# Identity transposes in unread PSUM banks at eight further places of a decoder stack

## What is computed

```python
# L0_ffn, two iterations of refining (names shortened)
logits = gelu(x @ w_r1 + b_r1) @ w_r2 + b_r2            # router, 8 experts, top 2
ctrl   = shared(ctx) + sum_k share_k * expert_k(ctx)    # ctx = [x, v]; alpha, beta, gate
x_next, v_next = step(ctrl, x, v, mu)
halt   = sigmoid(gelu(x_next @ w_h1 + b_h1) @ w_h2 + b_h2)
x, v   = blend by halt of x_next + iw * (gelu(x_next @ w_f1 + b_f1) @ w_f2 + b_f2)
# L1_xattn: 16 heads, each (batch, head) with a temperature from a small net
#           over mean, variance and maximum of its scores
# L1_ffn: top-1 of 14 experts: tokens sorted by expert, expert MLP, rows put back
```

## Time and profile before

| | |
|---|---|
| three timed executions | 1138.63, 1141.52, 1149.40 us (median 1141.52) |
| profiled execution, its own time | 1149.13 us |
| its span, first to last instruction | 1147.0 us |
| PE busy | 958.3 us (84%) |
| DVE, ACT, POOL busy | 749.4, 580.3, 418.2 us |
| mean granted PE clock | 0.92 of full |

### The profile page before, as it was taken

How to read it: one execution, slowest core, us unless ns; L and a number is a source line. 1 busy time by engine, 2 the same in 40 slices (tenths; PEclk the granted TensorE clock), 3 DMA queues, 4 the chain that set the end, 5 groups by cost and what they waited for, 6 DMA issues and landing times. The chain is left out here.

```text
span 1147.0 us, 27427 instructions
## 1 busy us (share of the span) xinstructions
PE 958.3 (84%) x11169; PEld 658.4 (57%) x11169; DVE 749.4 (65%) x2045; ACT 580.3 (51%) x960; POOL 418.2 (36%) x436
## 2 busy tenths in 40 slices
PE   8999899999899988988897694876657676689997
PEld 5677544444444445776686393444556565557776
DVE  4687776547756474653575143589999999646764
ACT  3565565645455435644562561476554645325442
POOL 4320300000000022776001666256778778623341
PEclk8899898999999998999797897898878888799999
DMA  7000000000000016000000223000000000000001
GB/s 277 2 3 3 20 1 1 1 1 0 1 1 1 0 62 244 3 3 2 2 3 1 84 76 117 6 1 1 2 3 3 2 2 3 2 1 2 3 2 38
DMA packets 16299, 27.98 MB, mean 24 GB/s; under 512 B 1200, under 2 KB 13616, under 8 KB 15664
## 3 DMA queue, kind: packets, MB, share of 16 engines
q1 hardware_dynamic: 14720, 23.09, 5.7%
q0 software_dynamic: 1024, 2.10, 0.6%
q10 hardware_dynamic: 432, 1.05, 0.3%
HBM read 20.33 MB, written 5.90 MB: 23 GB/s over the span
## 5 line engine op out<-in xcount | busy, mean ns | idle before, releaser
L1435 PE MATMUL l0f_ctl<-l1f_in,l0f_in 128*128 128x512 f32 x320 | 145.6, 598 | 0.0
L134 POOL TENSOR_SCALAR row_var_eps<-row_mean_var 128x4 f32<-128x4 f32 (+1 forms) x20 | 4.5, 225 | 360.4 <-DVE row_mean_var L129 359.6
L631 DVE TENSOR_REDUCE l_neg_max<-l_ring 128x4 f32<-128x512 f32 x128 | 82.0, 682 | 48.5 <-PE l_ring L444 48.2
L575 ACT ACTIVATE l_probs<-l_scores 128x1024 f32<-128x1024 f32 x64 | 65.5, 1023 | 80.8 <-PE l_scores L452 80.8
L1435 PEld LDWEIGHTS l0f_ctl<-l1f_in,l0f_in 128*128 128x128 f32 x320 | 61.8, 193 | 70.3 <-issue 68.1
L2864 ACT COPY l2f_blocks_sb<-l2f_right_t_sb 32x1024 f32<-32x1024 f32 x64 | 66.8, 1044 | 67.7 <-PE l2f_given_ps L2789 35.0
L2789 PE MATMUL l2f_given_ps<-l2f_blocks_sb,l2f_left_t_sb 128*32 128x128 f32 x1024 | 47.9, 364 | 32.1 <-ACT l1f_in L2870 20.6
L797 POOL TENSOR_TENSOR l_squares<-l_exps 128x1024 f32<-128x1024 f32 x32 | 60.6, 1893 | 27.9 <-ACT l_exps L1053 27.9
L1145 DVE TENSOR_REDUCE l_neg_max<-l_scores 128x8 f32<-128x1024 f32 x32 | 39.2, 1225 | 43.4 <-PE l_scores L849 43.4
L2789 PEld LDWEIGHTS l2f_given_ps<-l2f_blocks_sb,l2f_left_t_sb 128*32 128x32 f32 x1024 | 42.1, 148 | 44.2 <-issue 44.0
L398 POOL TENSOR_SCALAR_AFFINE_SELECT l_probs<-l_probs 128x1024 f32<-128x1024 f32 x32 | 34.9, 1092 | 61.4 <-ACT l_probs L575 61.4
(11 more groups left out here) (489 smaller groups left out, 2697.1 us busy)
## 6 DMA issues: line engine op xcount, KB each, us to landing
l1f_in<-in_l1f SPq DMA_DIRECT2D x1, 4580.0 KB, 13.7
l0f_in<-in_l0f SPq DMA_DIRECT2D x1, 2304.0 KB, 8.6
l0f_in<-in_l2f SPq DMA_DIRECT2D x1, 2080.5 KB, 19.3
l1f_in<-in_l2u SPq DMA_DIRECT2D x1, 2048.0 KB, 8.7
sorted_rows<-first_in SPq DMA_DIRECT2D x1, 1856.0 KB, 11.5
l1f_sorted<-sorted_rows SPq DMA_DIRECT2D x7, 256.0 KB, 4.2
expert_rows<-l1f_sorted SPq DMA_DIRECT2D x7, 256.0 KB, 2.2
l_in<-in_l SPq DMA_DIRECT2D x1, 962.5 KB, 11.7
```

The source lines that it names most:

```text
L575: nc.scalar.activation(probs[c % 2][:, 2 * pair:2 * pair + 2], scores2[:, :, :, :, :], ACT.Exp, scale=SCORE_SCALE).then_inc(exp_done, 1)
L631: ring.free(V.tensor_reduce(out, score_bank(b, half, g), AX.X, ALU.max, negate=True), ("score", b, half, g))
L1435: return nc.tensor.matmul(out, lhs, rhs, start=start, stop=stop)
```

## The change

98 transposes of the identity are added on PE, at eight points of the program, by the same helper:

- tempered attention: 12 between `project(1)` and the first row transposes;
- refining, router: 6 ahead of the four router matmuls, and 6 behind them, both into `ctl` bank 5;
- refining, `ask` of (0, 0) and of (0, 2): 8 ahead of the wait for `x_next`, into the bank of the halting matmuls, and 14 between `refine_a` and `refine_b`, into the `ctl` bank of the part that comes next. Ahead of the 14 PE waits until that bank is free (`ctl.wait_free`), a wait that before stood only ahead of the part itself;
- top-1: 30 ahead of `turn(0)`, into the bank of the router's logits.

```diff
             for n in range(AHEAD):
+                if n == T:
+                    turn_identity(nc, m, scores1[:, 1, 0, 0, :], 12)
                 if n in (T, 2 * T):
...
+    WAITED_FOR = ((0, 0), (0, 2))
...
             def route_all(it, c):
                 name = f"route_{it}{c}"
                 work.wait_free(pe, name, 0)
+                turn_identity(nc, m, ctl.banks[5][:, 0:S], 6)
                 for k in range(NCH):
                     norm.wait_stored(pe, k)
                     ins = mm(work.bank(name)[32 * k:32 * k + 32, :], w["w_r1"][:, :], features(k))
                 work.fill(ins, name)
+                turn_identity(nc, m, ctl.banks[5][:, 0:S], 6)
                 work.wait_freed(pe, name, 0)
...
-            def ask(it, c):
+            def ask(it, c, n, g):
                 name = f"halt_h_{it}{c}"
                 work.wait_free(pe, name, 0)
                 if (it, c) == CONTROLS[-1]:
                     turn_identity(nc, m, work.bank(name)[:, 0:S], 26)
+                if (it, c) in WAITED_FOR:
+                    turn_identity(nc, m, work.bank(name)[:, 0:S], 8)
                 pe.wait_ge(next_made, phase(it, c) + 1)
...
                 for k, name in enumerate(("refine_a", "refine_b")):
                     name = f"{name}_{it}{c}"
+                    if k == 1 and (it, c) in WAITED_FOR:
+                        key = (n,) + PARTS[CONTROLS[n][0]][g]
+                        ctl.wait_free(pe, key, 0)
+                        turn_identity(nc, m, ctl.bank(key)[:, 0:S], 14)
                     work.wait_free(pe, name, 0)
...
+            turn_identity(nc, m, logits_ps.rearrange("p b e -> p (b e)")[:, 0:S], 30)
             turn(0)
```

More of the change, by code:

```diff
@@ L1541, in stages @@
                 for stage, it, c in beside(n, g):
-                    if stage != "rank":
+                    if stage == "ask":
+                        ask(it, c, n, g)
+                    elif stage != "rank":
                         {"route": route_all, "hide": hide, "choose": choose, "spread": spread, "share": share_out,
-                         "ask": ask, "answer": answer, "again": again, "finish": finish}[stage](it, c)
+                         "answer": answer, "again": again, "finish": finish}[stage](it, c)
             for i in range(NCH):
```

## The result

Over 20 timed executions each, the median went from 1141.09 to 1134.3 us. The ratio is 0.9944, with a 95% interval from 0.9921 to 0.9967: a gain of 6.4 us, between 3.8 and 9.0. The forecast was 1136.5 us, a gain of 5.0. The ratio leaves out the executions that lie over 1.5% above the fastest of their kernel, one on each side; the medians alone differ by 6.8 us. Single executions of the changed kernel spread from 1126.65 to 1144.25 us and those of the kernel before from 1133.54 to 1152.27, so each kernel's own spread, some 18 us, is three times the effect.

The account below looks back on a forecast made before the run. PE, busy 958.3 of 1147.0 us and not always at full clock, bounds most stretches. Terms -1.6 + 0.8 - 3.6 - 2.2 = -6.6, taken as -5.0 for a median run: 1141.5 - 5.0 = 1136.5 us, range 1130 to 1142.5.

Parts of the forecast that it names:

- Rival 1: All places: the transposes do not hold the clock, so the change is 0, 1141.5 us; chance 0.08.
- tempered: Start of tempered attention: 3.40 us of PE work at half clock halves, -1.6 us, bounds 0 and -1.7.
- router: Refining's router: no gain, slow stretch moves from 130 to about 139 us, behind the choice; +0.8, bounds -0.3 and +2.8.
- asks: Asks (0, 0) and (0, 2): half-clock work halves, -4.0 together, less a tenth: -3.6 us, bounds 0 and -4.0.
- top-1: Top-1: 5.03 us busy at half clock shrinks, -2.2 us, bounds -1 and -2.5.
- The tenth that I took off for other engines: Asks: gaps of 6.0 us behind them, where other engines decide, could swallow savings; -4.0 cut to -3.6.
- Rival 3: Refining layer, 181 to 314 us: waits for ACT's weights and GELU swallow the asks' part, 1139.0 us; chance 0.23.
- Cover: All places: the added transposes, 0.12 us each at full clock, fit in PE's idle time and cost nothing.
- The undiscounted -6.6: Whole kernel: sum of the four terms against the profiled execution, giving 1142.5 us for it.
- the discount: Median run has fewer slow stretches: tempered counted -1.1, asks -2.5, top-1 and router unchanged; -5.0 instead of -6.6.
- Rival 2: All places: all of the gain passes and nothing moves at the router, -8.5, 1133.0 us; chance 0.20.
- Rival 4: Top-1, asks, tempered: transposes overrun their gaps at low clock, 0.215 us each, +5.8, 1147.3 us; chance 0.05.

Follow-up runs that it names:

- the kernel with the filled gap: The changed kernel with 22 more turns ahead of PE's wait for DVE's choice rows of (0, 0) at the router; ratio 0.9928 [0.9892, 0.9964] against the kernel before.

## Why the prediction was right

**The mechanism.** The changed kernel's clock is at 1.00 at both asks, at tempered's start and at top-1, with the transposes in the idle time. Rival 1, that transposes do not hold the clock, is out: in the kernel with the filled gap 22 transposes carried full clock over a gap of 2.8 us. The Trainium skill, "TensorE: Matmul & The Clock Gate", section "Part 4: PE-mode transpose", has it that full clock does not engage for transposes; for those issued here that does not hold.

**The terms**, as forecast and as measured, in this pair of profiles except for the second ask:

| term | forecast | measured | what it is measured by |
|---|---|---|---|
| tempered | -1.6 | -1.70 | step to the first scores |
| router | +0.8 | +0.86 | step to the first expert part |
| asks | -3.6 | -2.6 and -1.4 | step behind the first; the second below |
| top-1 | -2.2 | -2.17 | step to the last expert matmul |
| sum | -6.6 | -7.0 | |

Just ahead of the second ask the changed kernel's profile has another fall, from 285.5 to 288.9 us (the +0.96 and part of the -0.66 in the table), and with it the two steps together are 0.3 us longer than before. In the six other profiles with the 14 turns there and no such fall they are 84.3 and 54.5 us, against 84.3 and 55.9: -1.4. That fall stands in two of the eight profiles with the 14 turns and in none of the five without, which is too few to call it chance or the change's.

*Router.* This was the term that looked most like a gain, 6.8 us at half clock, and it was the one forecast as a loss. Both halves held: the step to the choice is 15.66 us with and without, and the slow stretch came back at 135.3, behind a gap of 2.81 us that was put at 2.4 to 3.8. The size varies from run to run, 0.5 to 1.3 us, with the place of the fall: 1.30 in the two profiles where it began some 0.5 us ahead of the choice, 0.86 and 0.94 where it began 0.5 and 0.4 us behind it, 0.64 at 0.7 and 0.48 at 1.2. The forecast of +0.8 was chosen between -0.3 and +2.8 and not worked out, so its closeness is luck; the sign and the place are not.

*Asks.* The tenth that I took off for other engines was not needed. From `refine_b` of the second and of the third phase's ask to the ask that follows it took 35.80 and 41.86 us in both kernels, to 0.01 us, so what was gained at the first ask was passed on. Rival 3 is out: the gaps of 6 us did not swallow anything. Over all profiles the step to the second phase's ask is 55.28 to 55.31 us in the eight with the 14 turns, and 57.87, 58.01, 57.05, 56.98 and 55.30 in the five without.

*Top-1.* The step from the first sorted group to the last expert matmul is 30.57 to 30.63 us in the nine profiles with turns there and 32.59, 32.79, 32.96 and 33.02 in the four without.

*Cover.* At tempered, at the asks and at top-1 the turns stayed in their gaps, and so did the six behind the router's matmuls. The six ahead of them did not, and here the prediction read its row wrongly. The row puts 1.01 us of idle time down to ACT's store, but PE's own list takes as long: between the last row transpose and the router it has eight semaphore increments (lines 1549 and 1551), which the trace has from 126.84 to 127.98 us, about 0.15 us apart. The six turns stand behind these in the list and not beside them. So the router's matmuls began 5.01 to 5.05 us behind the first row transpose in the six profiles with these turns, and 4.38 to 4.42 in the seven without, 0.6 us late. That cost nothing only because DVE sets the choice; it is luck and not cover. 0.12 us each was a little high, since a dense row runs at 0.109.

**From one profile to the median.** Here the step was right in kind, and -5.0 stands against -6.4 in the ratio, inside its interval of 3.8 to 9.0. The undiscounted -6.6 lies inside it too, so the totals do not tell whether the discount was right. I discounted the profiled stretches because executions differ by where the clock falls. Runs show that this is so: in the four profiles of kernels without turns at the asks, both asks fell but for one first ask, which was spared (55.30 us); tempered's start fell in two of the four profiles without turns. Taking the asks at their full -3.6 would have given -6.1, which is closer.

**Rival 2** (all passes and nothing moves at the router) is out by the router's step. **Rival 4** did not occur where it was looked for: `x_next`, `refine_b` and the sorted group are still released by DVE, ACT and a DMA.

## What to carry to other kernels

Filler on the throttled engine pays where three things are true together: the clock falls there, the engine is on the path while it is low, and the filler ends before the release. Read all three from the profile, and look also at what the engine's own list does in the gap, since idle time that it spends on semaphore increments is not there for work that stands behind them. A long slow stretch beside a busy DVE is worth nothing, and filling the gap ahead of it can push the slow stretch to a place where it costs. Where single executions spread by 18 us, compare the same step in several profiles, as 0.9 us is then plain to see, and never take the difference of two profiled executions for the effect.

## What the runs showed that was not expected

How much of a gap must be filled was not to be guessed. At top-1 half of the turns, with 1.98 us left idle, held the clock in the one profile; at the asks, 8 turns ahead and 2.37 us idle behind did not, and the 14 behind without the 8 did. At the start of the first layer one fall lasted 17 us with PE busy 16.09 of them, and the executions with it began the second block some 6 us later (123.8 and 123.7 against 117.2 to 119.2 us). Two more, with a fall of 10.2 us at the same place, began it at 121.3 and 121.9 us. That one place is as large as the whole change.
